# The last finish of an attention and mixture-of-experts kernel, regrouped: gates transposed instead of products, dense and routed sums apart, bias on GpSimd

## The reference

```python
def _L0_attn_ref(x, w_qkv, w_out):            # 2048 tokens, width 128, 16 heads of 8
    ...
    attn = jax.nn.softmax(scores, axis=-1)     # causal, with rotary embedding
    out = jnp.einsum('bhqk,bhkd->bhqd', attn, v)
    return out.transpose(0, 2, 1, 3).reshape(B, S, D) @ w_out
...
def _L0_ffn_ref(x, ...):
    base_out = einsum('bsi,oi->bso', x, base_W) + base_b
    shared_out = einsum(einsum('bsi,ri->bsr', x, shared_A), shared_B)      # rank 16
    logits = jnp.einsum('bsi,ei->bse', x, router_W) + router_b             # 6 experts
    gate = jax.nn.softmax(logits, axis=-1)
    topk_w, topk_i = jax.lax.top_k(gate, K)                                # K = 2
    sparse_w = ... / (jnp.sum(sparse_w, axis=-1, keepdims=True) + 1e-06)
    h = jnp.einsum('bsi,eri->bser', x, routed_A)                           # rank 16 each
    routed_out = einsum(einsum(h, routed_B), sparse_w)
    return base_out + shared_out + routed_out
...
x = x + _L0_attn_ref(_layernorm(x), ...)
x = x + _L0_ffn_ref(_layernorm(x), ...)
```

## Time and profile before

| what | value |
|---|---|
| median of 3 runs | 298.48 us (298.29 to 298.51) |
| the profiled execution | 298.24 us, of which the span from first to last instruction is 296.5 us |
| granted clock of TensorE | 1.000 of full speed on average |
| busy over the span | PE 94%, ACT 90%, DVE 47%, POOL 22% |
| from 284.6 to 288.4 us | PE busy 3.67 of 3.80 us |
| from 288.4 to 292.4 us | PE busy 3.97 of 4.00 us, fillers included |
| from 292.4 us to the end | PE busy 1.47 of 4.10 us |

### The profile page before, as it was taken

The page is one execution under the profiler, slowest core; times in us unless marked ns, Lnnn a source line. Parts: engine busy times, 40 slices in busy tenths (PEclk is TensorE's granted clock), DMA queues, the critical chain, the costliest instruction groups (busy, mean ns, idle before and its releaser), DMA issues.

```text
span 296.5 us, 7512 instructions
## 1 busy us (share of the span) xinstructions
PE 279.1 (94%) x3002; PEld 102.4 (35%) x3002; DVE 139.6 (47%) x420; ACT 267.3 (90%) x303; POOL 65.4 (22%) x145
## 2 busy tenths in 40 slices
PE   7869989899999999999999999999999999999996
PEld 2624332222132222122233124445433435445343
DVE  6876866687141558526171036522113262541054
ACT  8647899899999999999998999999999998999910
POOL 3576455514304012040030121010101010103000
PEclk9999999999999999999999999999999999999999
DMA  6443434004610000000000700001000001000000
GB/s 204 116 103 88 128 90 128 0 3 107 155 59 2 4 0 2 0 0 2 2 0 18 214 22 2 2 2 38 0 3 2 2 3 35 2 2 2 21 0 18
DMA packets 15256, 11.75 MB, mean 40 GB/s; under 512 B 2081, under 2 KB 14226, under 8 KB 15218
## 3 DMA queue, kind: packets, MB, share of 16 engines
q1 hardware_dynamic: 14594, 10.64, 13.0%
q0 software_dynamic: 192, 0.39, 0.5%
q10 hardware_dynamic: 432, 0.20, 0.3%
HBM read 3.88 MB, written 1.05 MB: 17 GB/s over the span
## 4 chain that ended last, share of the span: by engine, by line
PE 49%; ACT 25%; issue 14%; DVE 8%; DMA 2%; SPq 0%; ACTq 0%; DVEq 0%
ACT pbuf L713 24%; PE po L1147 22%; PE ps L1124 13%; PE ps L1270 2%; PE ps L1163 2%; PE pm L1163 1%; PE pm L1208 1%; PE pm L1157 1%; DMA qst<-parts 1%; PE pm L1169 1%; PE pm L1214 1%; PE pm L1222 1%; DVE rest L797 1%; DMA xs<-x_dram 1%; PE pm L1218 1%
## 5 line engine op out<-in xcount | busy, mean ns | idle before, releaser
L713 ACT ACTIVATE pbuf<-ps 128x1024 f32<-128x1024 f32 (+1 forms) x280 | 253.8, 1074 | 12.0 <-PE ps L1124 11.2
L1147 PE MATMUL po<-pbuf,va 128*9 128x256 f32 (+3 forms) x1792 | 143.8, 426 | 1.5 <-DVE oq L777 1.0
L1124 PE MATMUL ps<-qst,kst 64*128 64x256 bf16 (+3 forms) x896 | 97.6, 297 | 7.6 <-ACT pbuf L713 3.1
L649 POOL TENSOR_SCALAR_AFFINE_SELECT pbuf<-pbuf 128x256 f32<-128x256 f32 (+1 forms) x104 | 47.7, 481 | 196.4 <-ACT pbuf L713 195.2
L1124 PEld LDWEIGHTS ps<-qst,kst 64*128 64x128 bf16 x896 | 30.4, 94 | 106.3 <-ACT pbuf L713 80.5
L1147 PEld LDWEIGHTS po<-pbuf,va 128*9 128x9 f32 x1792 | 35.2, 89 | 55.9 <-issue 33.9
L777 DVE STREAM_TRANSPOSE oq<-po 128x256 f32<-128x256 f32 (+1 forms) x24 | 12.9, 538 | 65.4 <-PE po L1147 65.2
L1270 PE MATMUL ps<-kst 128*128 128x512 bf16 x46 | 11.3, 380 | 1.2 <-issue 1.2
L797 DVE TENSOR_TENSOR rest<-pm,sinT 32x512 f32<-32x512 f32 x16 | 11.0, 687 | 0.3
L1163 PE MATMUL ps<-xnT,wqkv 128*128 128x256 f32 (+1 forms) x24 | 8.3, 470 | 0.2 <-ACT xnT L683 0.2
L744 DVE BATCH_NORM_STATS2 stats<-xs 128x6 f32<-128x128 f32 x32 | 7.1, 281 | 2.4 <-DMA xs<-x_dram 1.3
(11 more groups left out here) (156 smaller groups left out, 186.3 us busy)
## 6 DMA issues: line engine op xcount, KB each, us to landing
qst<-parts SPq DMA_DIRECT2D x18, 128.0 KB, 2.8
kst<-parts SPq DMA_DIRECT2D x18, 128.0 KB, 2.6
xs<-x_dram SPq DMA_DIRECT2D x4, 256.0 KB, 3.3
cosT<-rope_c_dram SPq DMA_DIRECT2D x3, 256.0 KB, 4.0
sinT<-rope_s_dram SPq DMA_DIRECT2D x3, 256.0 KB, 4.5
out_dram<-xs SPq DMA_DIRECT2D x3, 256.0 KB, 2.3
kst<-parts SPq DMA_DIRECT2D x8, 64.0 KB, 2.2
qst<-parts SPq DMA_DIRECT2D x7, 64.0 KB, 2.5
```

Source lines behind the costliest of these rows:

```text
L649: ins = nc.gpsimd.affine_select(out=edge, in_=edge, compare_op=ALU.is_ge, fill=0.0, base=0, pattern=[[0, edge.shape[1]], [1, P]], channel_ ...
L713: nc.scalar.activation(probs[:, :, 0:width], ps[:, SLOT[u], :, 0:width], ACT.Exp, scale=SCALE).then_inc(exp_ready, 1)
L1124: ins = nc.tensor.matmul(ps[:, SLOT[u], e, place:place + n], side(kst, e)[:, g * 2 + pair, key:key + P], side(qst, e)[:, g * 2 + pair, q:q ...
L1147: ins = nc.tensor.matmul(po[32 * j:32 * j + DH + 1, q0:q0 + n], va[:, kt, g * GH + j, :], pbuf[:, u % NPB, at:at + n], start=blk["first"] ...
```

## The change

The finish of the last two tiles is regrouped.

- `w_down` and `w_up` have their columns and rows in another order: routed 96 first, then shared 16.
- PE: router columns alone for each tile (6 columns, into `pm`); then one product with `wdown` as the weights, so that the 112 low-rank values come out already transposed, for both tiles at once (into `po`); then the base products; then, after ACT's copy of `po` into `lowT` (tiles 2 and 3 of it), the shared terms (16 rows) complete the dense banks. Five fillers. Then the kept gates (96 columns, each gate repeated 16 times) are transposed, two fillers, and the routed products go into banks of their own.
- ACT: the copy of `po`; the exponential; the dense banks times `rstd`, into `ln`.
- POOL: `ln` = x + `ln` for each tile, then x = `ln` + bias for each tile (`bbias`, a new tile of 128x128, loaded by one more DMA on SP's queue after `rbias`; so the waits on `ffn_in` are for 6 transfers and not 5). The column of the deviation is gone.
- DVE: the comparison L980 is put ahead of the difference for the exponential; the kept gates are not normalised but written out repeated; turned gates are multiplied into `lowT`; the reciprocal of the sum, times `rstd`, becomes the factor of the last instruction, which is routed bank times factor plus what POOL left.
- At the first flag: three bfloat16 fillers and one of float32 with 512 columns, for four bfloat16 fillers.

```diff
-WARM_O, WARM_X, WARM_R, WARM_U, WARM_F = 8, 7, 2, 14, 2
+WARM_O, WARM_X, WARM_R, WARM_U, WARM_F = 8, 7, 2, 5, 2
 TIE = 1e-30
 TIE_BLOCK = max(b for b, block in enumerate(BLOCKS) if block["last"] and block["i"] == NPIECE - 2)
 WARM_START = 16
 WARM_BOUND = 6
-WARM_FLAG = 4
+WARM_FLAG = 3
...
-            for dst, src in ((wout, w_out), (wdown, w_down), (wup, w_up), (wbase, w_base), (rbias, router_b)):
+            for dst, src in ((wout, w_out), (wdown, w_down), (wup, w_up), (wbase, w_base), (rbias, router_b),
+                             (bbias, base_b)):
...
-            pool.wait_ge(end_scale, 1)
-            nc.gpsimd.tensor_tensor(low_rank[:, 0:END_TILES, RD], var[:, 0, 0:END_TILES], rstd[:, 0, 0:END_TILES],
-                                    ALU.mult).then_inc(end_deviation, 1)
+            for t in range(END_TILES):
+                pool.wait_ge(end_scaled, t + 1)
+                nc.gpsimd.tensor_tensor(ln[:, t, :], xs[:, END + t, :], ln[:, t, :], ALU.add).then_inc(end_summed_up, 1)
+            pool.wait_ge(ffn_in, 16 * 6)
+            for t in range(END_TILES):
+                pool.wait_ge(end_summed_up, t + 1)
+                nc.gpsimd.tensor_tensor(xs[:, END + t, :], ln[:, t, :], bbias[:, :], ALU.add).then_inc(end_biased, 1)
...
+            act.wait_ge(end_down, 1)
+            nc.scalar.copy(lowT[0:RD, 2:2 + END_TILES, :].rearrange("p t d -> p (t d)"),
+                           po[0:RD, 0:END_TILES * P]).then_inc(end_low, 1)
             act.wait_ge(end_logits, 1)
             nc.scalar.activation(gate[:, 0:END_TILES, :], above[:, 0:END_TILES, 0, :], ACT.Exp).then_inc(end_exp, 1)
-            by_tile = pm[:, 0:END_TILES * P].rearrange("p (t d) -> p t d", t=END_TILES)
-            nc.scalar.copy(low_rank[:, 0:END_TILES, 0:R], by_tile[:, :, 0:R]).then_inc(end_shared, 1)
-            act.wait_ge(end_low_turned, 2)
-            nc.scalar.copy(lowT[0:RD + 1, 1, :], po[0:RD + 1, 0:P]).then_inc(end_low_last, 1)
+            act.wait_ge(end_scale, 1)
+            for t in range(END_TILES):
+                act.wait_ge(end_dense, t + 1)
+                nc.scalar.activation(ln[:, t, :], dense_banks()[t], ACT.Copy, scale=rstd[:, 0, t:t + 1]).then_inc(end_scaled, 1)
...
+                dve.wait_ge(end_raw, 1)
                 mine, top, less = lg[:, 0:nt, :], chosen[:, 0:nt], above[:, 0:nt, 0, :]
                 for t in range(nt):
-                    ins = nc.vector.scalar_tensor_tensor(lg[:, t, :], by_tile[:, t, RD:RD + E], scale[:, t:t + 1],
+                    ins = nc.vector.scalar_tensor_tensor(lg[:, t, :], by_tile[:, t, 0:E], scale[:, t:t + 1],
                                                          rbias[:, :], ALU.mult, ALU.add)
                 then(ins)
-                then(nc.vector.tensor_reduce(top, mine, AX.X, ALU.max))
-                nc.vector.tensor_tensor(less, mine, top.unsqueeze(2).broadcast_to([P, nt, E]),
-                                        ALU.subtract).then_inc(end_logits, 1)
                 shape = [P, nt, E, E]
                 this, other = mine.unsqueeze(3).broadcast_to(shape), mine.unsqueeze(2).broadcast_to(shape)
                 lead, over = ties[:, 0:nt], end_over[:, 0:nt]
-                then(nc.vector.tensor_tensor(lead, other, this, ALU.subtract))
+                topped = step(nc.vector.tensor_reduce(top, mine, AX.X, ALU.max))
+                led = step(nc.vector.tensor_tensor(lead, other, this, ALU.subtract))
+                dve.wait_ge(vec, topped)
+                nc.vector.tensor_tensor(less, mine, top.unsqueeze(2).broadcast_to([P, nt, E]),
+                                        ALU.subtract).then_inc(end_logits, 1)
+                dve.wait_ge(vec, led)
                 then(nc.vector.scalar_tensor_tensor(over, lead, -1.0, tie_first[:, :, :].unsqueeze(1).broadcast_to(shape),
                                                     ALU.mult, ALU.is_lt))
                 then(nc.vector.tensor_reduce(rank[:, 0:nt, :], over, AX.X, ALU.add))
                 dve.wait_ge(end_exp, 1)
                 kept, total, share = rank[:, 0:nt, :], small[:, 0:nt], gate[:, 0:nt, :]
+                for t in range(nt):
+                    nc.vector.scalar_tensor_tensor(low_rank[:, t, 0:RT].rearrange("p (e r) -> p e r", e=E),
+                                                   kept[:, t, :].unsqueeze(2).broadcast_to([P, E, R]), 1.5,
+                                                   share[:, t, :].unsqueeze(2).broadcast_to([P, E, R]),
+                                                   ALU.is_lt, ALU.mult).then_inc(end_kept, 1)
                 nc.vector.tensor_reduce(total, share, AX.X, ALU.add)
-                then(nc.vector.scalar_tensor_tensor(kept, kept, 1.5, share, ALU.is_lt, ALU.mult))
-                then(nc.vector.tensor_reduce(top, kept, AX.X, ALU.add))
-                then(nc.vector.scalar_tensor_tensor(total, total, 1e-6, top, ALU.mult, ALU.add))
-                then(nc.vector.reciprocal(total, total))
-                then(nc.vector.tensor_tensor(share, kept, total.unsqueeze(2).broadcast_to([P, nt, E]), ALU.mult))
-                dve.wait_ge(end_shared, 1)
-                nc.vector.tensor_tensor(low_rank[:, 0:nt, R:RD].rearrange("p t (e r) -> p t e r", e=E),
-                                        by_tile[:, :, R:RD].rearrange("p t (e r) -> p t e r", e=E),
-                                        gate[:, 0:nt, :].unsqueeze(3).broadcast_to([P, nt, E, R]),
-                                        ALU.mult).then_inc(end_routed, 1)
-                dve.wait_ge(end_low_turned, 1)
-                nc.vector.tensor_copy(lowT[0:RD + 1, 0, :], pm[0:RD + 1, 0:P]).then_inc(end_low, 1)
+                dve.wait_ge(end_kept, nt)
+                then(nc.vector.tensor_reduce(top, low_rank[:, 0:nt, 0:RT:R], AX.X, ALU.add))
+                normal = step(nc.vector.scalar_tensor_tensor(total, total, 1e-6, top, ALU.mult, ALU.add))
+                dve.wait_ge(end_low, 1)
                 for t in range(nt):
+                    dve.wait_ge(end_gates, t + 1)
+                    nc.vector.tensor_tensor(lowT[0:RT, t, :], gate_banks()[t], lowT[0:RT, 2 + t, :],
+                                            ALU.mult).then_inc(end_gated, 1)
+                    if t == 0:
+                        dve.wait_ge(vec, normal)
+                        turned = step(nc.vector.reciprocal(total, total))
+                dve.wait_ge(vec, turned)
+                then(nc.vector.tensor_tensor(total, total, scale[:, 0:nt], ALU.mult))
+                for t in range(nt):
+                    dve.wait_ge(end_biased, t + 1)
                     dve.wait_ge(end_full, t + 1)
-                    nc.vector.scalar_tensor_tensor(xs[:, END + t, :], last[t][:, 0:P], scale[:, t:t + 1], xs[:, END + t, :],
+                    nc.vector.scalar_tensor_tensor(xs[:, END + t, :], routed_banks()[t], total[:, t:t + 1], xs[:, END + t, :],
...
                 keep_warm(WARM_R, *hot)
                 pe.wait_ge(end_input, 1)
                 for t in range(END_TILES):
-                    ins = nc.tensor.matmul(pm[:, t * P:t * P + RD + E], feat[:, tile(t)], wdown[:, :], start=True, stop=True)
-                ins.then_inc(end_down, 1)
+                    ins = nc.tensor.matmul(pm[:, t * P:t * P + E], feat[:, tile(t)], wdown[:, RD:RD + E], start=True, stop=True)
+                ins.then_inc(end_raw, 1)
+                nc.tensor.matmul(po[0:RD, 0:END_TILES * P], wdown[:, 0:RD], feat[:, 0:END_TILES * P],
+                                 start=True, stop=True).then_inc(end_down, 1)
                 for t in range(END_TILES):
-                    nc.tensor.matmul(end_banks()[t][:, 0:P], feat[:, tile(t)], wbase[:, :], start=True, stop=False,
+                    nc.tensor.matmul(dense_banks()[t], feat[:, tile(t)], wbase[:, :], start=True, stop=False,
                                      skip_group_check=True)
+                pe.wait_ge(end_low, 1)
+                for t in range(END_TILES):
+                    nc.tensor.matmul(dense_banks()[t], lowT[RT:RD, 2 + t, :], wup[RT:RD, :], start=False, stop=True,
+                                     skip_group_check=True).then_inc(end_dense, 1)
                 keep_warm(WARM_U, *hot)
-                pe.wait_ge(end_shared, 1)
-                pe.wait_ge(end_deviation, 1)
-                pe.wait_ge(end_routed, 1)
                 for t in range(END_TILES):
-                    nc.tensor.transpose((pm, po)[t][0:RD + 1, 0:P], low_rank[:, t, 0:RD + 1],
-                                        idf[:, :]).then_inc(end_low_turned, 1)
+                    pe.wait_ge(end_kept, t + 1)
+                    nc.tensor.transpose(gate_banks()[t], low_rank[:, t, 0:RT], idf[:, :]).then_inc(end_gates, 1)
                 keep_warm(WARM_F, *hot)
-                for t, ready in enumerate((end_low, end_low_last)):
-                    pe.wait_ge(ready, 1)
-                    nc.tensor.matmul(end_banks()[t][:, 0:P], lowT[0:RD + 1, t, :], wup[:, :], start=False, stop=True,
```

(14 more changed lines are left out.)

43 lines of the change are left out of this document (26 added, 17 removed).

## The result

Median 297.67 us (297.28 to 298.39, 14 runs) against 298.34 us before (298.12 to 298.80, 14 runs): ratio 0.9978, 95% interval 0.9971 to 0.9986, so 0.4 to 0.9 us faster. 297.5 us had been predicted, a gain of 0.97 us; 0.67 was measured.

The account below looks back on a forecast made before the run. Exponentials and products bind the body (PE 94%, ACT 90%), untouched; PE fillers bind the tail. Terms -0.97 + 0 + 0 = -0.97 us, so 298.48 - 0.97 = 297.5 us; range 297.1 to 298.7.

Parts of the forecast that it names:

- Fillers bind, gates just behind: Tail of the kernel before: PE's fillers, not VectorE's gates, set the start of the gate transposes, by 0.13 us.
- Router products 0.46, nearest to the loads of 128 columns: PE, start of tail: four 6-column instructions take 0.46 us, since each still loads 128 columns of weights.
- the rival of cheap router products: PE, start of tail: router products take 0.1, so the end comes 0.36 earlier, 297.15 us; chance 0.10.
- 256-column product 0.43, shared products 0.46: PE before the five fillers: the 256-column product streams 0.43 us, the shared products stream 0.46 us.
- VectorE's chain: VectorE up to the kept gates: rank ends 0.20 earlier, gates near 290.91 and 291.07, ahead of PE at 291.51.
- Behind the transposes: Tail after the gate transposes: 0.33, 0.29, 0.06 and 0.53 us to VectorE's first result; end 293.32 against 294.30.
- GpSimd, p = 0.43: GpSimd in the tail: one 128-column addition (p) takes 0.43 us; the fourth ends at 292.54, hidden.
- the rival that built on them: GpSimd takes the wait's place: additions of 0.80 give 298.6 us, 0.93 give 299.1, from 128-column scalings; chance 0.15.
- The new transfer: SP queue at the start: 0.57 us issue delays the first stack by 0.26; hidden, 0; uncovered, 0.26.
- The first flag, 0 on the time: PE near the start: float32 filler adds 0.83 us of work, but an instruction fetch ends the gap; 0.
- the rival with a held-up read: First flag is read only when the fillers have ended: scores about 0.4 late, 297.9 us; chance 0.10.
- Sum: Whole kernel: tail -0.97, new transfer 0, first flag 0, together -0.97 us.

Follow-up runs that it names:

- experiment 2: Kernel before with 5 fillers of WARM_U instead of 14, nothing else: finish 9.68 us, median 298.54 us, ratio 0.9995 (the run b_u5).
- a_rows: Changed kernel with shared terms made from all 112 rows instead of 16: products to fillers 0.54, finish 9.03, one run of 297.65 us.
- a_wait: a_first with waits on GpSimd and the factor moved to an empty instruction ahead of VectorE's last two: finish 9.02, one run of 297.43 us.
- a_best: a_lean with GpSimd's early bias additions started one step sooner: finish 8.39, median 296.88 us, ratio 0.9955.
- experiment 6: Changed kernel with bias first, waits moved to empty instructions and two fillers, as a_lean (finish 8.61) and a_best (finish 8.39).
- b_u5: Kernel before with 5 fillers of WARM_U instead of 14, nothing else: finish 9.68 us, median 298.54 us, ratio 0.9995.
- a_noflag: Changed kernel with four bfloat16 fillers and no float32 one at the first flag: finish 9.13, median 297.86 us, ratio 0.9986.
- a_first: Changed kernel with GpSimd adding the bias first, leaving one addition per tile behind ACT's scaling: finish 9.13, one run of 297.70 us.
- a_lean: a_wait with two fillers of WARM_U and the wait for ACT's copy moved off the first multiplication: finish 8.61, 297.13 us, ratio 0.9951.

## Why the prediction was right, and what was mis-sized

- *Fillers bind, gates just behind.* Right for the changed kernel: fillers more or fewer move the end nearly one for one (11.08, 9.14, 8.53). For the kernel before it was misread: by the working, cutting fillers alone would give 0.13; it gives 0.00 (experiment 2), because the load for the transposes starts 0.11 and the transpose itself 0.15 behind the gates, not 0.05. The sum did not use that 0.13, so it is none of the missing 0.43.
- *Router products 0.46, nearest to the loads of 128 columns.* The number is right to the hundredth and the reason holds, but the exactness is in part luck. They too stand behind a wait, which made it 0.54 at L1289, and that 0.08 shows one step later. With that the rival of cheap router products is out.
- *256-column product 0.43, shared products 0.46.* Too small by 0.08 and 0.18: the largest misses. For the first, the loads of the step behind the wait, before and after:
```profile
288.90 0.53 PEld L1292 LDWEIGHTS ps<-wbase,feat 128*128 128x128 f32 x4
289.11 0.28 PEld L1326 LDWEIGHTS po<-feat,wdown 128*112 128x112 f32 x2
```
Both start 0.44 behind the first load of the step ahead (288.46 and 288.67), so four loads take as long for 6 columns as for 118. But L1292's product starts 0.10 behind its load and L1326's only 0.02 (289.13), and of L1326's two instructions the first takes 0.29 (to 289.42) and the second 0.22 (to 289.64). So I read the 0.08 as again that of a first load behind a wait, showing one step late. No run tests it alone. The second miss is shown: 0.10 for the loads behind the few rows (a_rows), and the 0.08 for the first load behind a wait stands in both a_rows and L1289.
- *VectorE's chain.* `rank` 0.20 earlier, gates at 291.07: measured 291.29 - 0.21 = 291.08. The gates' slack was put at 0.4 and is 0.7, since PE came later.
- *Behind the transposes.* Carried over as 0.33 and 0.53, measured 0.38 and 0.64. I counted what each instruction computes and not that it now waits for two or three events. The 0.11 is shown by a_wait. That the 0.05 is such a wait too is not shown; a_best, which was to show it, had another instruction in the way.
- *GpSimd, p = 0.43.* Measured 0.87 for two: one record is 0.46 long and the next starts 0.41 behind it, so the four take 1.70 and not 1.72. Rows 6 were no guide to it, and the rival that built on them is out. Its start was 0.26 late (0.08 at the shared products' start, 0.05 to ACT, 0.13 at ACT, where one scaling takes 0.37 and not 0.27), still with 0.62 of slack. The Trainium skill ("GPSIMD Engine Reference", section 3.1) led to an estimated 0.48; the trace is a little below. Its section 8, contention with VectorE instructions of two inputs in the same memory, which I had left without a price, agrees with L463 in experiment 6 (0.16 to 0.37). L475 has one input and was stretched too (0.17 to 0.32). Together it is 0.35 us for 0.87 us of additions.
- *The new transfer.* Mis-sized, rightly dropped: its issue took 1.17 and not 0.57 (30.49), and the first stack went out 1.4 later (31.78 against 30.36 in the earlier trace rows). The body is 266.13 and 266.14 us in two kernels without it and 266.14 to 266.23 in eight with it. Outside stand b_u5, whose clock fell (266.70), and a_noflag (266.67), where PE waited 0.46 longer for VectorE at 53.6 us: one of VectorE's instructions beside GpSimd's masks took 0.42 and the next four 1.49, against 0.16 and 1.29 in the changed kernel.
- *The first flag, 0 on the time.* Right for the median and in the mechanism, and the rival with a held-up read is out (17.31 against 17.40). The reason that I gave for full clock in that gap, one profile, was too little: in 13 of 80 executions it did not hold.
- *Sum.* -0.97 predicted, -0.54 in the finish of the profiled execution, -0.67 between medians. The difference between the last two is within what the interval leaves open. Part of it can be the filler at the flag, for which I had put 0: with it alone the old kernel's median is 0.14 lower, and without it the changed kernel's 0.19 higher, both within the noise.

## What to carry to other kernels

Where one engine runs through the tail in program order, fillers and a slow chain bind together: measure the slack of each, then cut both, since cutting one may give nothing. When a step is regrouped, price not only what the instructions compute but what they wait for: a first weight load behind a wait, loads that are not taken ahead behind a product of few rows, and further events on one instruction were about 0.1 us apiece here and took 0.4 of a 0.97 us gain. Look at the granted clock of many executions before calling a filler useless.

## What the runs showed of the hardware that was not expected

- Float32 products on rows 96 to 111 cost more than on rows 0 to 111 when another product follows: 0.64 against 0.54 for two, the next weights loaded only at 290.90 with their own product.
- GpSimd additions of 128 columns (0.87 for two) stretch VectorE's smallest instructions: 0.17 to 0.32 and 0.16 to 0.37 (a_first), 0.16 to 0.30 (a_best against a_lean).
- TensorE, idle in both cases, starts 0.06 behind the end of the instruction that releases it where it waits for one event (L1304), and 0.15 where it waits for three (L1299 in b_u5); VectorE starts 0.11 to 0.12 later with three events than with one (a_first against a_wait).
- The clock falls to 0.50 in some executions after the same 1.2 to 1.4 us gap that leaves it at 1.00 in others; a float32 product of 512 columns in the gap, 0.83 us more of work, kept it at 1.00 in 56 of 56 to within 0.002.
